# One signal for four products instead of two for two: handing a slot's messages to TensorE in a graph attention kernel

## The reference, cut to what matters

```
h  = (x @ W).reshape(N, 8, 32)
e  = leaky_relu(el[src] + er[dst])          # el, er: one number per node and head
ex = exp(e - m[dst])                        # weight of an edge, per head
s  = segment_sum(ex, dst)
out = segment_sum(h[src] * (ex / s[dst]), dst)
```

## Time and profile before

| | |
|---|---|
| median of the runs | 9743.75 us |
| the profiled execution, by the same clock as the runs | 9719.24 us |
| its span, first to last instruction | 9717.4 us |
| mean granted TensorE clock | 0.803 of 2.4 GHz |
| busy: TensorE / VectorE / GpSimd / ScalarE | 65% / 52% / 46% / 20% |
| aggregation matmuls, L1249 | 3667.1 us busy |
| selections, L963 | 1565.3 us busy |
| messages, L972 | 1732.2 us busy |

### The profile page before, as it was taken

One profiled execution on the slowest core, in us unless ns is written; L12 is line 12 of the kernel. 1 busy time (PEld: TensorE's weight loads), 2 busy tenths in 40 slices (PEclk: granted clock), 3 DMA queues, 4 the chain that ended last, 5 costly groups with the idle time before them and its releaser, 6 DMA issues.

```text
span 9717.4 us, 172782 instructions
## 1 busy us (share of the span) xinstructions
PE 6287.2 (65%) x38910; PEld 4899.6 (50%) x38911; DVE 5020.9 (52%) x14572; ACT 1955.3 (20%) x5913; POOL 4475.7 (46%) x4723
## 2 busy tenths in 40 slices
PE   3555555666666455555556566455777888889899
PEld 2434444444444333434444444334566667777778
DVE  4444555555555454555555566444554555555554
ACT  1000000101111000000000000001333444555555
POOL 0555554544444555555444444455444443333332
PEclk8677777777787676777777777777888899999999
DMA  4443433433333344333333333443333232222221
GB/s 157 109 106 99 103 101 101 106 96 98 99 100 93 102 106 99 101 101 98 98 97 97 98 98 96 94 104 99 92 89 83 78 78 76 74 72 70 66 67 44
DMA packets 638578, 909.85 MB, mean 94 GB/s; under 512 B 271425, under 2 KB 484554, under 8 KB 638410
## 3 DMA queue, kind: packets, MB, share of 16 engines
q0 software_dynamic: 226368, 676.39, 26.8%
q1 hardware_dynamic: 369546, 192.99, 8.4%
q10 hardware_dynamic: 42624, 40.02, 1.2%
HBM read 868.05 MB, written 40.87 MB: 94 GB/s over the span
## 4 chain that ended last, share of the span: by engine, by line
PE 28%; issue 18%; another core or an unknown queue 16%; DVE 15%; DVEq 12%; DMA 4%; ACT 4%; SPq 2%; ACTq 1%; POOL 1%; POOLq 0%
PE bank L1249 17%; DVE msg L972 6%; PE bank L1177 5%; PE bank L1188 4%; DVE sel L963 4%; DMA dstb<-dst_d 3%; DVEq L237 3%; DVEq L963 1%; DVE lg L955 1%; ACT region L429 1%; ACT L466 1%; DVEq L943 1%; DVEq L955 1%; SPq L328 1%
## 5 line engine op out<-in xcount | busy, mean ns | idle before, releaser
L353 POOL DMA_INDIRECT gat<-table,meta x4716 | 4474.7, 949 | 5152.8 <-SPq L335 3529.1
L1249 PE MATMUL bank<-msg,sel 128*128 128x264 f32 x10560 | 3667.1, 506 | 1751.7 <-DVE msg L972 1335.7
L1249 PEld LDWEIGHTS bank<-msg,sel 128*128 128x128 f32 x10560 | 2482.9, 247 | 2375.9 <-DVE msg L972 1432.7
L963 DVE TENSOR_SCALAR sel<-kc,base_i,meta 128x128 f32<-128x128 f32 x5280 | 1565.3, 355 | 1470.0 <-remote 799.9
L972 DVE TENSOR_TENSOR msg<-gat,bank 128x528 f32<-128x528 f32 x2640 | 1732.2, 697 | 576.5 <-ACT bank L473 480.2
L471 ACT ACTIVATE ex<-lg 128x32 f32<-128x32 f32 x1320 | 298.8, 226 | 6040.5 <-DVE lg L958 4609.5
L1225 PE MATMUL bank<-uvb,selT 128*128 (+1 forms) x15876 | 672.1, 172 | 1166.5 <-DVE selT L943 681.4
L1225 PEld LDWEIGHTS bank<-uvb,selT 128*128 128x128 bf16 x15876 | 617.0, 100 | 1566.9 <-issue 932.0
L955 DVE TENSOR_TENSOR lg<-gat,bank 128x64 f32<-128x64 f32 x1320 | 288.9, 219 | 1712.0 <-remote 901.4
L1177 PE MATMUL bank<-xT,w 128*128 128x128 f32 x6272 | 790.9, 281 | 18.0 <-issue 18.0
L1188 PE MATMUL bank<-w,region 128*128 128x256 f32 x3136 | 773.6, 390 | 42.2 <-ACT region L429 24.4
(11 more groups left out here) (184 smaller groups left out, 2435.7 us busy)
## 6 DMA issues: line engine op xcount, KB each, us to landing
dstb<-dst_d SPq DMA_DIRECT2D x1179, 128.0 KB
gat<-table,meta POOLq DMA_INDIRECT x4716
meta<-in_edges SPq DMA_DIRECT2D x1179, 4.0 KB
table<-hrow ACTq DMA_DIRECT2D x98, 140.0 KB
w<-in_W SPq DMA_DIRECT2D x2, 4096.0 KB
table<-hrow SPq DMA_DIRECT2D x49, 140.0 KB, 1.8
region<-xnT_d ACTq DMA_DIRECT2D x50, 128.0 KB
region<-qT_d ACTq DMA_DIRECT2D x50, 128.0 KB
```

The costliest lines, as they stand in the source:

```text
L353: pool.indirect_dma_start(gat[:, r, c, :], None, table[l], bass.IndirectOffsetOnAxis(meta[:, r, c, 0:1].bitcast(U32), 0)).then_inc(s_done, 16)
L963: dve_v.tensor_scalar(sel[:, c, :], iota, base_i[:, bass.ds(T, 1)], meta[:, bass.ds(g % RING, 1), c, 1:2].rearrange("p a w -> p (a w)"), A ...
L1249: last = pe.matmul(acc[:, 0:MSG], sel[:, c, :], msg[:, c, :], start=False, stop=False)
```

## The change

The halves go. `messages` issues one `tensor_tensor` over all four groups (4 x 264 = 1056 columns) with one increment of `msg_ready`; `aggregate` waits once and runs its four matmuls, of which the last increments `agg_done` once; `logits` waits once for the whole aggregation of the slot before and then builds all four selections. The counts in SyncE's wait and in the starting values follow: the slot that SyncE waits for is the same one.

```
-        HALF = CH // 2
-        AHEAD = 2 * RING
+        AHEAD = RING
...
-                        sp.wait_ge(msg_ready[l], 2 * (g + shift) + 2)
+                        sp.wait_ge(msg_ready[l], g + shift + 1)
...
-                dve.sem_inc(agg_done[l], 2)
+                dve.sem_inc(agg_done[l], 1)
...
-                    for h in range(2):
-                        dve.wait_ge(agg_done[l], 2 * n + h + 1)
-                        for c in range(h * HALF, (h + 1) * HALF):
-                            dve_v.tensor_scalar(sel[:, c, :], iota, base_i[:, bass.ds(T, 1)],
-                                                meta[:, bass.ds(g % RING, 1), c, 1:2].rearrange("p a w -> p (a w)"),
-                                                ALU.add, ALU.is_equal)
+                    dve.wait_ge(agg_done[l], n + 1)
+                    for c in range(CH):
+                        dve_v.tensor_scalar(sel[:, c, :], iota, base_i[:, bass.ds(T, 1)],
+                                            meta[:, bass.ds(g % RING, 1), c, 1:2].rearrange("p a w -> p (a w)"),
+                                            ALU.add, ALU.is_equal)
...
-                    for h in range(2):
-                        cs = slice(h * HALF, (h + 1) * HALF)
-                        dve_v.tensor_tensor(
-                            msg[:, cs, :].rearrange("p c (h d) -> p c h d", h=H),
-                            rows_of(g)[:, cs, 0:MSG].rearrange("p c (h d) -> p c h d", h=H),
-                            ex_p[:, cs, :].unsqueeze(3).to_broadcast([P, HALF, H, D + 1]), ALU.mult).then_inc(msg_ready[l], 1)
+                    dve_v.tensor_tensor(
+                        msg[:, :, :].rearrange("p c (h d) -> p c h d", h=H),
+                        rows_of(g)[:, :, 0:MSG].rearrange("p c (h d) -> p c h d", h=H),
+                        ex_p.unsqueeze(3).to_broadcast([P, CH, H, D + 1]), ALU.mult).then_inc(msg_ready[l], 1)
...
-                    for h in range(2):
-                        pe.wait_ge(msg_ready[l], 2 * n + (AHEAD + h + 1))
-                        for c in range(h * HALF, (h + 1) * HALF):
-                            last = pe.matmul(acc[:, 0:MSG], sel[:, c, :], msg[:, c, :], start=False, stop=False)
-                        last.then_inc(agg_done[l], 1)
+                    pe.wait_ge(msg_ready[l], n + (AHEAD + 1))
+                    for c in range(CH):
+                        last = pe.matmul(acc[:, 0:MSG], sel[:, c, :], msg[:, c, :], start=False, stop=False)
+                    last.then_inc(agg_done[l], 1)
```

## The result

The kernel after the change takes 9643.12 us (median of 4 runs, 9635.17 to 9666.15); the kernel before, on the same chip, 9745.04 us (4 runs, 9727.61 to 9778.39). The ratio is 0.9895 with a 95% interval of 0.9864 to 0.9927: about 1% faster. The forecast was 5.1% slower.

What follows compares the result with a forecast made beforehand. It took a one-buffer ring between VectorE and TensorE, plus late TensorE signals, as the bound. 493 us for longer turns, less 37 for removed work, plus 43 for the clock, gave +499 us: 10,240 us, 5.1% slower, range 9,860 to 10,660.

Steps and rivals of the forecast that it cites:

- The turn: One round of selections, messages and aggregation: grows 1.05 us, 3.47 to 4.52 at full clock, 5.32 to 6.37 at half.
- The message instruction: VectorE's single 1056-column message instruction: 1225 ns, so TensorE starts 0.53 us later and VectorE is free 0.085 us earlier.
- the rule of the Trainium skill: VectorE's messages: merging saves a fixed latency per instruction, 169 ns a slot; if all were won, 9521 us.
- How many turns pay: Slots where VectorE's selections wait for the aggregation: 470 at 1.05 us each, 493 us, bounds 325 and 860 us.
- the 320 late ones: The selections' remote waits, 799.9 us in the profile, counted as waits for TensorE's aggregation signal.
- the ring: One-buffer loop between VectorE and TensorE (selections, messages, aggregation, selections), forecast to get 1.05 us longer a turn.
- the forecast's own other terms: Besides the turns: 37 us less for VectorE's removed work, 43 us more for TensorE's lower clock.
- The bound of 860 us: Upper bound for the turns: all 819 aggregation waits for messages pay 1.05 us each.
- A: Rival on TensorE's signals: late signals absorb the change, +124 us, 9868 us; chance 0.16.
- B: Rival on TensorE's signals: fewer signals, fewer stalls, -147 us, 9597 us; chance 0.09.
- C: Rival on TensorE's clock: half the warm slots in the ring go cold, +1119 us, 10,860; chance 0.14.
- P: Theory from the experiments, not the prediction: the longer ring spaces out gathers or work, so fewer signals are held; no chance given.

Runs made afterwards that it cites:

- r_after_again: The changed kernel, unaltered, run on chip 11, where signals come on time: 8729.59 us, 1.1253 of the kernel before.
- c_extra_signal: The changed kernel, but TensorE signals after two and after four products and VectorE waits once, for the second: 9763.59 us, 0.9868 of the kernel before.
- g_two_waits: The changed kernel with two aggregation signals and two VectorE waits, one behind the other, ahead of all four selections: 9683.69 us, 0.9963 of the kernel before.
- d: The changed kernel with messages in two instructions of 528 columns, signalling after the second alone: 9805.97 us, 0.9921 of the kernel before.
- a: The kernel before with the four selections merged behind one wait and one aggregation signal, messages still in halves: 9772.66 us, 0.9866 of the kernel before.
- b: The changed kernel with selections and TensorE's signal in halves again, the message instruction staying single: 9876.15 us, 0.9989 of the kernel before.
- n: The kernel before with 0.7 us of idle additions on VectorE in each slot, on chip 8: 9943.22 us, 1.0049 of the kernel before.
- m: The changed kernel with two message buffers, messages made ahead of the wait and the selections after it: 10079.85 us, 1.0167 of the kernel before.
- o: The kernel before with a memset and a drain on GpSimd ahead of each slot's gathers, on chip 8: 9933.57 us, 1.0026 of the kernel before.

## Why the prediction was wrong

*The turn: right.* 4.56 us at full clock for 4.52, 6.38 us at half clock for 6.37.

*The message instruction: right.* This is its group after, x1320:

```profile
L968 DVE TENSOR_TENSOR msg<-gat,bank 128x1056 f32<-128x1056 f32 x1320 | 1645.5, 1247 | 631.6 <-ACT bank L472 511.1 <-issue 120.4
```

1247 ns for 1225. The removed fixed part was 2 x 697 - 1247 = 147 ns by the rows, but 1.31 - 1.25 = 0.06 us on the engine. Merging messages alone gave 0.9989, so the rule of the Trainium skill that was weighed there ("VectorE: DVE Perf Modes", "The TRN2 errata — SBUF-src ops pay a fixed extra latency per instruction") did not carry the gain; the 9521 us that it would have given are not seen.

*How many turns pay: this step failed.* The forecast put 470 x 1.05 = 493 us on the end: 310 slots for the 619 waits that ended with TensorE, and 160 more for the 320 remote ones, since "the 320 late ones are waits for the same signal". They are, but a late signal is not one that comes a fixed time after the aggregation; it comes when something lets it go. That took away more than the share of the 160 slots (168 us): the 310 alone, 325 us, would still have made the kernel slower. The forecast added every lengthened turn to the end and left the 1701.3 us of remote waits as they were, a change of nothing in the main sum. In place of that, the remote waits of layers 0 and 1 fell by 593 us as the ring grew, and work added to VectorE on such a chip costs 48 us where it costs 705 us with signals on time. Where signals come on time the same step is wrong in the other direction: the change costs 968 to 985 us there, about (985 + 37 - 43) / 1.05 = 932 turns by the forecast's own other terms, and the selections' wait ended with TensorE 1049 times (`r_after_again`). The bound of 860 us from the 819 waits was nearer to that than the value I took.

*Rivals.* A (the late signals absorb the change) named the mechanism; its 9868 us left 310 slots paying, and they did not on balance. B (fewer signals, fewer stalls, 9597 us) has the sign and is 46 us off, but its reason fell: `c_extra_signal` keeps both signals and gains as much. Its second half, one wait in place of two, has the larger part: with the second wait `g_two_waits` keeps a gain of only 0.4%, and of what it loses 47 us (36 ns a slot) is the price of the wait and its signal where nothing is held. The remark against B, that both halves were late one after the other, was the thing to price: the remote waits of the selections fell by 45%, 799.9 to 436.1 us.

*C, the clock: right in sign, too small in size.* The mean time of a slot's eight records went from 2.78 to 2.99 us:

```profile
L1244 PE MATMUL bank<-msg,sel 128*128 128x264 f32 x10560 | 3951.3, 537 | 2356.9 <-DVE msg L968 2018.2 <-issue 338.4
```

That is 284 us more of aggregation than in the earlier trace rows, where 43 was put and 259 was the upper bound. It is busy time, and how much of it reached the end is not shown; granted clock 0.73, 0.71 and 0.87 for 0.75, 0.74 and 0.89.

*Sum.* On a chip with signals on time the forecast had the sign and half the size (499 us for 985). On the chip of the comparison it had the wrong sign, since its profile held 1701 us of remote waits, of which I priced the selections' as ring and kept all fixed.

**What stays open.** Why the hold is shorter in the kernel after. Lateness is 1.3 to 1.5 us in the four kernels in which no selection or message lies beside an aggregation (the changed kernel and runs `c`, `d`, `g`) and 2.1 to 2.4 in those where one does (before and runs `a`, `b`, `n`, `m`). It is also low with the pause (`o`, 1.47 us), whose time did not fall, and high in `a` (2.30 us), whose time did. The pause is bound by GpSimd, but `g`, at 1.34 us, also gains only 0.4%. So the time does not follow this number alone, and the gain of `a` is shown but not explained. In layers 0 and 1 the gathers come in fewer long bursts after the change (14 bursts over 11 us, 37 before; 633 of mean 5.82 us, 512 of 7.18), which goes with P; that it is the cause is argued, not shown, and the difference hangs on what is called a burst: if gaps of up to 2 us are counted into it, there are 168 and 165 over 11 us. What in the chip holds the signals, and why chips differ, no view shows: nothing of the program differs between the two kinds. One rival stands untested, the recording of the trace. Where signals are held many rises have no record: 331 of ScalarE's 1320 in the trace before, 7 in `r_after_again`. Those signals were not late, for where VectorE sat waiting it began 0.14 us after ScalarE's end with or without the record, but the recording too goes otherwise there, and no run tells what the hold is without it. A second buffer for the selections too was not tried. Of the parts, only the second wait was tried on both kinds of chip, and `a` and `c`, as fast as the change where signals are held, never where they come on time. Between the two kernels, before is the one to take where signals come on time (7759 us for 8744), after where they are held.

## What to carry to other kernels

When a wait is "remote" or its releaser had long ended, find out first whether it grows with what stands before it; add a known 0.7 us there, and if the time stays, do not price the wait as part of a ring. And run the kernel on more than one chip: an edit worth -1.7% on one costs 12.7% on another here, and a kernel tuned on the first kind has been tuned around the stall. A profile whose engines are all half idle and whose turns, counted in the timeline, are shorter than the mean slot (3.47 and 5.32 for 6.66 us) is a reason to look for it, and no proof: with signals on time the changed kernel's mean slot in layer 0 is 2471 / 440 = 5.62 us with turns of 4.56 and 6.38. Last, measure what a test edit does before reading its result: the pause meant as 1 us was 2.9 us long and moved the bound to GpSimd.

## What the hardware showed that I had not expected

- TensorE's completion signals for the logits came 2.40 us late on average in the kernel before, 5% of them over 8 us, and on time (0.01 us) once GpSimd had issued no gather for 3 us. They were late on chips 8, 12, 14 and that of the first comparison; on chips 6 and 11 they came within 0.01 us. The kernel before takes 9729 to 9895 us on the one kind and 7759 to 7762 on the other.
- On the first kind SyncE's two DMA issues of a slot lay 0.93 us apart on average in the kernel before, in 1% of the slots 2.9 us or more; on the second kind they lay 0.55 us apart.
- Leaving out three gathers of four took 21% off the time of a kernel whose GpSimd is busy for 46%.
- Work of 0.7 us a slot on VectorE cost 48 us in 9895 on the one kind and 705 us in 7759 on the other.
- A memset of 0.97 us with a drain behind it kept GpSimd from its next gather for 2.8 to 2.9 us, on both kinds.
- A second wait with its signal, already met when it is reached, cost 36 ns a slot on VectorE.
